# A Perceiver block on one Trainium2 core: the expert stage reordered, part of it moved into the last layer, and one exchange in the layers

## The reference, cut to what matters

```python
x = x + xattn(ctx, layernorm(x))
x = x + eight_layers(layernorm(x))        # attention part, then an MLP 512 -> 2048 -> 512, each with a layer norm
y = layernorm(x)
# 32 groups of 16 tokens; 64 experts (NE=16 times ES=4), each with 64 hidden units
logits = grouped(y) @ controller + tie
perm = (logits == max over the 16 tokens of a group)      # each expert picks one token of each group
sel = perm^T @ grouped(y)
inner = relu(sel @ f1 + bias)
inter = inner @ f2
out = perm @ inter                        # given back to the token that was picked
x = x + out
```

## Time and profile before

| | |
|---|---|
| median of 3 runs | 2298.01 us (2297.53 to 2298.12) |
| the profiled execution | 2295.51 us, of which the span from first to last instruction is 2293.7 us |
| PE busy | 94% of the span |
| DVE, ACT, POOL busy | 73%, 48%, 42% |
| mean granted TensorE clock | 0.984 of full speed |
| expert stage, first DVE instruction to the end | 2172.19 to 2293.7, 121.5 us |

### The profile page before, as it was taken

The page is one execution under the profiler, slowest core; times in us unless marked ns, Lnnn a source line. Parts: engine busy times, 40 slices in busy tenths (PEclk is TensorE's granted clock), DMA queues, the critical chain, the costliest instruction groups (busy, mean ns, idle before and its releaser), DMA issues. The chain is left out here.

```text
span 2293.7 us, 37795 instructions
## 1 busy us (share of the span) xinstructions
PE 2158.8 (94%) x12735; PEld 1091.0 (48%) x12735; DVE 1672.0 (73%) x2402; ACT 1101.9 (48%) x1720; POOL 969.0 (42%) x651
## 2 busy tenths in 40 slices
PE   5899999989999999998999999999999999999758
PEld 2444444433333333322475655657575665757333
DVE  7687777669999999999566757566675756666672
ACT  4122223234444545554564646556564655656343
POOL 0244344369999999876222204022221302122140
PEclk9999999999999999999999999999999999999979
DMA  3344544332432333321324232333423333332230
GB/s 116 134 141 145 180 142 156 128 111 86 131 103 83 119 108 106 112 81 56 122 93 133 94 115 84 129 102 117 132 74 111 101 117 96 129 120 86 84 111 19
DMA packets 159851, 252.71 MB, mean 110 GB/s; under 512 B 11506, under 2 KB 63986, under 8 KB 159730
## 3 DMA queue, kind: packets, MB, share of 16 engines
q1 hardware_dynamic: 159730, 250.96, 34.2%
HBM read 211.73 MB, written 36.70 MB: 108 GB/s over the span
## 5 line engine op out<-in xcount | busy, mean ns | idle before, releaser
L66 PE MATMUL l_mm<-l_xt_hi,wt_hi 128*128 128x256 f16 (+3 forms) x1568 | 413.8, 275 | 18.6 <-ACT hf L1691 11.5
L1335 POOL TENSOR_TENSOR l_rstd<-l_var_eps,neg_half 128x1 f32<-128x1 f32 x68 | 65.7, 966 | 839.1 <-DVE l_var_eps L1387 839.1
L67 PE MATMUL l_mm<-l_xt_lo,wt_hi 128*128 128x256 bf16 (+3 forms) x1568 | 413.5, 275 | 0.0
L68 PE MATMUL l_mm<-l_xt_hi,wt_lo 128*128 128x256 f16 (+3 forms) x1568 | 413.1, 275 | 0.0
L995 ACT ACTIVATE probs<-sc 128x1024 f32<-128x1024 f32 x272 | 275.7, 1023 | 251.7 <-PE sc L1086 197.8
L867 POOL TENSOR_TENSOR h_lo<-h_lo,probs 128x896 f32<-128x896 f32 x136 | 290.3, 2135 | 23.2 <-ACT probs L995 11.9
L867 POOL TENSOR_TENSOR wt_lo<-wt_lo,probs 128x896 f32<-128x896 f32 (+1 forms) x136 | 249.2, 1832 | 36.5 <-ACT probs L995 27.4
L1098 PE MATMUL pv<-probs,vb 128*64 128x512 f32 x1088 | 263.2, 605 | 0.0
L881 DVE TENSOR_REDUCE pmax<-mx 128x1024 f32 (+1 forms) x196 | 239.3, 1221 | 28.4 <-PE mx L1072 20.0
L68 PE MATMUL l_tok<-wt_hi,h_lo 128*128 128x512 f16 x576 | 218.3, 379 | 0.0
L1085 PE MATMUL sc<-q_hi,res 128*128 128x512 f16 x544 | 207.7, 382 | 9.2 <-ACT probs L995 7.2
(11 more groups left out here) (275 smaller groups left out, 3924.9 us busy)
## 6 DMA issues: line engine op xcount, KB each, us to landing
stage<-in_L_attn_Wf SPq DMA_DIRECT2D x64, 1024.0 KB, 5.2
keys<-wt_hi SPq DMA_DIRECT2D x136, 128.0 KB
res<-keys SPq DMA_DIRECT2D x68, 256.0 KB, 3.3
vb<-values SPq DMA_DIRECT2D x68, 256.0 KB, 5.6
stage<-in_ctx SPq DMA_DIRECT2D x16, 1024.0 KB, 9.8
values<-wt_lo SPq DMA_DIRECT2D x16, 1024.0 KB
stage<-in_L_ffn_f SPq DMA_DIRECT2D x16, 1024.0 KB, 5.3
res<-keys SPq DMA_DIRECT2D x68, 128.0 KB, 5.4
```

The costliest lines, as they stand in the source:

```text
L66: pe.matmul(out, lh, rh, start=first, stop=False, **kw)
L67: pe.matmul(out, lh, rl, start=False, stop=False, **kw)
L68: return pe.matmul(out, ll, rh, start=False, stop=last, **kw)
```

## The change

1. *Layers, all eight.* DVE does the biases of tiles 2 and 3 ahead of the low part of tile 1; ACT does gelu 2 ahead of the high part of tile 1; the four pieces of chunk F2+3 move on ACT behind `hidden(0)`, `hidden(1)` and `hidden(2)`.
2. *Last layer.* The transposes, high and low parts of tiles 0 to 2 are made there, of the stream normalised by a new `final_norm(t)`, and so are the high and low rows (`row_high`, `row_low`). The constants of the expert stage are loaded there too. Buffers are shared between stages for this (no instruction is added by that).
3. *Expert stage, head.* Only tile 3 is normalised, transposed and split. The logits come in two parts (tiles 0 to 2, then tile 3). The picks are copied by ACT, spread by POOL in two instructions a tile instead of by DVE in one; POOL clears tile 0's part ahead of that and the rest behind it.
4. *Second weights.* All eight low parts are POOL's, behind the clearing. ACT makes the high parts of chunks 4 to 7 between the quads 0, 2, 4 and 6.
5. *Back.* The transposes of the first eight quads stand inside the inner blocks, the copies of them on ACT too.
6. *Quads.* The selection is ordered so that a quad's rows 0 to 63 belong to tiles 0 and 1 and rows 64 to 127 to tiles 2 and 3. `expert_out` makes 32 output rows at a time, 12 products a quad; `give_back` uses 64 rows of the contraction in each of its eight products. The four stream tiles are added after all of them.

```diff
+LAST_F2 = {0: (0, 1), 1: (2,), 2: (3,)}
@@ layers_phase, DVE
+                def final_norm(t):
+                    dve.wait_ge(final_added, t + 1)
+                    tile_stats(stream_event(t), t, k.x_sb[:, t, :], EPS_OUTER)
+                    dve.wait_ge(rstd_done, stream_event(t) + 1)
+                    v.tensor_scalar(res[:, t, :], k.x_sb[:, t, :], mv[:, t, 0:1], rstd[:, t:t + 1],
+                                    ALU.subtract, ALU.mult).then_inc(normed, 1)
+                def row_low(t):
+                    dve.wait_ge(row_hi_done, t + 1)
+                    v.tensor_tensor(k.f_lo[:, t, :], res[:, t, :], k.f_hi[:, t, :], ALU.subtract).then_inc(row_lo_done, 1)
...
                     tile_shift(l, 1, bc_attn)
-                    low(m0 + 1, 1)
                     tile_bias(l, 2, attn_out[2], bc_attn)
                     tile_bias(l, 3, attn_out[3], bc_attn)
+                    low(m0 + 1, 1)
...
-                        if t and not last:
+                        if t:
                             low(m0 + TT + t - 1, t - 1)
+                        if t and last:
+                            row_low(t - 1)
...
+                            if t < TT - 1:
+                                final_norm(t)
@@ layers_phase, ACT
                     high(m0 + 0, 0)
+                    tile_gelu(l, 2)
                     high(m0 + 1, 1)
-                    tile_gelu(l, 2)
                     tile_gelu(l, 3)
-                    for n in range(4):
-                        chunk_piece(F2 + 3, n)
...
                         hidden(j)
+                        for n in LAST_F2.get(j, ()):
+                            chunk_piece(F2 + 3, n)
@@ layers_phase, PE
-                            if f == 10 and t and not last:
-                                transposes(m0 + TT + t - 1, t - 1)
+                            if f == 10 and t:
+                                transposes(m0 + TT + t - 1, t - 1, stream_event(t - 1) if last else None)
@@ expert_phase, SP
                 for m in range(2, 8):
-                    if 2 <= m < 6:
-                        sp.wait_ge(w_lo_pool, 4 * (m - 1))
-                    elif m >= 6:
-                        sp.wait_ge(w_lo_dve, 4 * (m - 5))
+                    sp.wait_ge(w_lo, 4 * (m - 1))
@@ expert_phase, POOL
-                g.memset(spread[:], 0.0).then_inc(cleared, 1)
+                clear(0)
+                for t in range(TT):
+                    spread_tile(t)
+                for t in range(1, TT):
+                    clear(t)
+                for m in range(8):
+                    weight_low(m)
@@ expert_phase, ACT
+                act.wait_ge(k.c_in, 48)
+                a.activation(ctl_hi[:], ctl[:], ACT.Copy).then_inc(ctl_hi_done, 1)
                 weight_high(0)
-                weight_high(1)
...
+                weight_high(1)
+                for b in range(BLOCKS_OF_PAIRS):
+                    back_copy(b)
                     act.wait_ge(inner_relu, b + 1)
                     a.activation(in_hi[:, 8 * b:8 * b + 8, :], inner[b % 2], ACT.Copy).then_inc(in_hi_done, 1)
-                    act.wait_ge(inner_ready, 4 * (b + 1))
-                    weight_high(4 + b)
+                    if b >= 2:
+                        weight_high(b)
+                for n in range(QUADS // 4, QUADS // 2):
+                    back_copy(n)
                 for q in range(QUADS):
...
                     a.activation(it_hi[q % 2], work[q % 2][:], ACT.Copy).then_inc(it_hi_done, 1)
+                    if q % 2 == 0 and q < 8:
+                        weight_high(4 + q // 2)
@@ expert_phase, PE
+                    if q % 2 == 0:
+                        pe.wait_ge(w_lo, 4 * (q // 2 + 1))
...
-                        x = product3(t_, work[q % 2][half * 64:(half + 1) * 64, :], (in_hi[:, pair, :], in_lo[:, pair, :]),
-                                     (wt_hi[:, m, n, :], wt_lo[:, m, n, :]), True, True)
+                        for a in range(2):
+                            rows, cols_ = slice(64 * a + 32 * half, 64 * a + 32 * half + 32), slice(32 * a, 32 * a + 32)
+                            x = product3(t_, work[q % 2][rows, :], (in_hi[:, pair, cols_], in_lo[:, pair, cols_]),
+                                         (wt_hi[:, m, n, :], wt_lo[:, m, n, :]), True, True,
+                                         tile_position=(0, rows.start))
...
-                    for t in range(TT):
-                        lhs = back[:, q, t * P:(t + 1) * P]
-                        t_.matmul(outs[t][:], lhs, it_hi[q % 2], start=q == 0, stop=False)
-                        x = t_.matmul(outs[t][:], lhs, it_lo[q % 2], start=False, stop=q == QUADS - 1)
+                    for part, it in enumerate((it_hi[q % 2], it_lo[q % 2])):
+                        for turn in range(2):
+                            for a in range(2):
+                                t = 2 * a + turn
+                                rows = slice(64 * a, 64 * a + 64)
+                                x = t_.matmul(outs[t][:], back(q)[rows, t * P:(t + 1) * P], it[rows, :],
+                                              start=q == 0 and part == 0,
+                                              stop=q == QUADS - 1 and part == 1)
```

More of the change, by code:

```diff
@@ L1712, in body @@
                             chunk_piece(F1 + t, n)
-                        if t and not last:
+                        if t:
                             high(m0 + TT + t - 1, t - 1)
+                        if t and last:
+                            row_high(t - 1)
                         tile_gelu(l, TT + t)
@@ L1890, in expert_phase, with back, packed @@
         outs = [pb(f"e_out{n}", [P, D], F32) for n in range(TT)]
-        c_in, staged = sem("e_c_in"), [sem(f"e_staged{n}") for n in range(2)]
+        logit_bank, pick_bank, bias_bank, tp_bank = outs
+        def back(q):
+            return back_early[:, q, :] if q < QUADS // 2 else back_late[:, q - QUADS // 2, :]
+        def packed(t):
+            return t[:].rearrange("p (e s g) -> p e s g", s=2, g=TILE_GROUPS)
+        staged = [sem(f"e_staged{n}") for n in range(2)]
         stats_done, mv_done, var_done, rstd_done, normed = (sem(n) for n in (
@@ L1936, in _, with clear, weight_low @@
                 g = nc.gpsimd
[L1937 to L1944 removed]
+                def clear(t):
+                    g.memset(spread[:, t, :, 1 - t // 2], 0.0).then_inc(cleared, 1)
+                    g.memset(spread[:, t, :, t // 2, :, 1 - t % 2], 0.0).then_inc(cleared, 1)
+                def weight_low(m):
                     pool.wait_ge(staged[m % 2], 16 * (m // 2 + 1))
@@ L1988, in _ @@
[L1988 to L1997 removed]
+                v.tensor_copy(bias_cols[:], bias_bank[:, 0:EP]).then_inc(bias_done, 1)
@@ new lines, in select @@
+                def select(t):
+                    pe.wait_ge(spread_done, 2 * t + 2)
+                    if t == LATE:
+                        pe.wait_ge(fr_lo_done, 1)
+                    for c in range(CH):
+                        n = CH * t + c
+                        if n >= 4:
+                            pe.wait_ge(sel_lo_done, n - 3)
+                        rhs = spread[:, t, :, t // 2, :, t % 2]
+                        out = work[n % 4][:].rearrange("p (q h n) -> p q h n", q=QUADS, h=2)
+                        t_.matmul(out, f_hi[:, t, c * P:(c + 1) * P], rhs, start=True, stop=False)
+                        t_.matmul(out, f_lo[:, t, c * P:(c + 1) * P], rhs, start=False, stop=True).then_inc(sel_ready, 1)
@@ L2131, in _ @@
                     x.then_inc(back_ready, 1)
+                pe.wait_ge(k.c_in, 48)
+                t_.transpose(bias_bank[:, 0:EP], k.bias_rows[:], k.ident[0:EP, 0:EP]).then_inc(bias_ready, 1)
+                pe.wait_ge(ctl_lo_done, 1)
+                logits_of(0)
+                pe.wait_ge(normed, 1)
+                for c in range(CH):
+                    x = t_.transpose(tp_bank[:, c * P:(c + 1) * P], f[:, LATE, c * P:(c + 1) * P], k.ident[:])
+                x.then_inc(tp_ready, 1)
@@ L2133, in expert_out @@
+                for n in range(QUADS // 4, QUADS // 2):
+                    back_transposes(n)
                 def expert_out(q):
+                    if q % 4 == 0:
+                        pe.wait_ge(in_lo_done, q // 4 + 1)
+                    if q % 2 == 0:
+                        pe.wait_ge(w_lo, 4 * (q // 2 + 1))
                     if q >= 2:
```

340 lines of the change are left out of this document (169 added, 171 removed).

## The result

The changed kernel takes 2260.54 us (median of 4 runs, 2255.57 to 2262.95), the kernel before on the same chip 2297.77 (2294.25 to 2298.12). The ratio is 0.984 with a 95% interval of 0.9822 to 0.9858: faster by 37.2 us. The forecast was 2262 in 2252 to 2276.

What follows compares the result with a forecast made beforehand. PE was taken to bound the layers, short chains, awaited weights and PE's quads the expert stage. Expert stage -36.5, last layer +9.4, layers -9.0 sum to -36.1: 2298.0 becomes 2261.9, predicted 2262 us, range 2252 to 2276.

Steps and rivals of the forecast that it cites:

- Layers, -9: Eight layers: PE's 1.44 us gelu wait goes, but tile 3's transposes lack slack; 1.1 gained a layer, bounds 0 to 11.5.
- rival D: Layers: the gain is eaten by tile 3's chain or ACT's later order, +9, 2271 us; chance 0.08.
- Last layer, +9.4: Last layer: PE stalls 2.7 us for the second norm plus transposes, 3.15 a tile, three tiles; bounds 1.4 to 12.
- Head, 9.4: Expert stage's start, up to the selection: 27.15 us becomes 9.4, -17.75; bounds 9 to 11.
- Selection, 12.2: Expert stage's selection: 11.86 us becomes 12.2; ACT gains one copy, PE starts at 1.2 GHz as before.
- Inner and back, 21.9: Expert stage's inner blocks and back transposes: 35.3 us becomes 21.9, -13.4; ACT's work sets the quads' start at 43.5.
- Quads, 36.3: Expert stage's sixteen quads: 43.3 us becomes 36.3, -7.0; 1.72 a quad, early ones held by ACT's queue and loads.
- the estimate of 0.84: Quads: `expert_out` would take 0.84 us by the skill's 3.07 times for four small tiles, making the whole 1.6 longer.
- B: Quads: small tiles overlap only partly: 64-row products not +7.4, 32-column products two at a time +5.7, both 2278 us; chance 0.17.
- E: Quads: small tiles run one after another, loads not hidden, 6.6 us a quad, kernel slower at 2332 us; chance 0.05.
- F: Quads: products serial, loads hidden, 4.52 us a quad, giving back what the rest gains, 2298 us; chance 0.04.
- rival C: Shorter: layers give all 11.5, head clock high, POOL 1.13 a piece: 2255 us, 2250 with half the stall; chance 0.08.

Runs made afterwards that it cites:

- e3: Changed kernel with only the layers' order of biases and gelu 2 (DVE and ACT) put back, weight pieces staying moved: 2271.81 us, ratio 0.9887.
- e2: Changed kernel with only the layers' weight pieces put back ahead of `hidden(0)` on ACT: 2261.29 us, ratio 0.984.
- e1: Changed kernel with both edits of the layers undone, on DVE and on ACT: 2270.81 us, ratio 0.9881.
- e5: Changed kernel with the last layer's transposes ahead of step 13 instead of step 10: 2257.19 us, ratio 0.9824.
- e9: Changed kernel with POOL clearing the first spread tile ahead of rstd instead of behind it: 2261.54 us, ratio 0.9844.
- e4: Changed kernel with `give_back` contracting all 128 rows instead of 64; 32-column products in `expert_out` kept: 2270.91 us, ratio 0.9879.
- e6: Changed kernel with ACT's weight chunks 6 and 7 moved from behind quads 4 and 6 to behind quads 6 and 9: 2259.0 us, ratio 0.9835.
- e7: Changed kernel with ACT's chunks 6 and 7 made in halves, two pieces behind each of quads 6 to 9: 2258.08 us, ratio 0.9828.
- e8: Changed kernel with 24 unused 512-column products added behind the layers' last product: 2259.88 us, ratio 0.9842.
- e13: Changed kernel with 29 unused products added behind the layers' last and 6 more ahead of the first logits: 2260.15 us, ratio 0.984.
- e11: Changed kernel with e5 and e7 together: 2251.3 us, ratio 0.9799.

## Why the prediction was right

Its mechanisms held, and nearly all its terms; the size came out with small errors that went both ways. The experiments undo or vary the layers, `give_back`, ACT's chunks and the last layer's stall. The two largest gains, head (17.7) and inner and back (12.6), no run undoes: for them the stretches of the two profiles stand alone.

- **Layers, -9.** PE's wait of 11.5 went, 3.4 came back at tile 3's transposes (4.4 less 1.0), and 0.8 less is waited elsewhere: 8.9, or 1.1 a layer as taken. Bias 0 is only 7.24 sooner, because the layers' first statistics are 0.63 later (1094.47 for 1093.84) and the clock behind them was lower (0.80 for 0.87), which the sum didn't have; like with like it is 8.8 to 9.0. The warning that tile 3 has no slack was the right one, and e3 shows it in full: rival D happens as soon as the order on DVE and ACT isn't changed too. Where I put the gain was half wrong: ACT's pieces ahead of `hidden(0)` looked like the cause, but moving them is neither needed (e2) nor enough (e3).
- **Last layer, +9.4.** Measured 9.8 (40.88 less 31.08). A tile grew by 2.70 instead of 3.15, as the stall is 2.07 and a little around it, not 2.7; that would be 8.1. The other 1.7 is the low clock in one of three tiles, which the sum didn't have. So that this term comes out is luck: a stall taken too long stood in for a low clock that was not foreseen, and with two such tiles, as in e1 and e3, it would be 11.5. In e5, where two waits of 0.93 are left, the low clock is gone.
- **Head, 9.4.** Measured 9.47, with the spread at 0.66 for 0.6 and the norm at 1.72 for the 0.55 used, which didn't matter, as e9 shows.
- **Selection, 12.2.** Measured 13.0: PE at 1.2 GHz for the first 5 us was slower than DVE's pace. The term's cover, "PE starts at 1.2 GHz as before", wasn't costed; it is 0.8 (in e9, where the clock rose sooner, the selection takes 11.8).
- **Inner and back, 21.9.** Measured 22.7.
- **Quads, 36.3.** Measured 35.2, but they began 1.7 later than forecast (45.2 behind the start for 43.5) and ended 0.6 later (80.4 for 79.8), because the loads and not the quads' beginning set their end. The chain through POOL's low parts and the loads came out closely: chunk 7 high at 64.3 behind the start (2239.01 less 2174.75) for 63.4, loads of 5.0 to 5.4, POOL 1.12 to 1.24 a piece. The steady period is 1.75 for 1.72. The 3.07 times and not four of the Trainium skill, TensorE: Matmul & The Clock Gate, Part 3, stands there for four tiles in rows, while `expert_out` has four in columns, so the estimate of 0.84 took it over to another kind; this trace shows no such loss, `expert_out` takes 0.65. Nor does a cost appear that would belong to a lost fast weight load (the Trainium skill, TensorEngine Tiling (Array Packing), Restrictions and Gotchas): the twelve loads hide behind twelve products.
- **End, 5.2.** Measured 5.2.

Expert stage 85.55 for 85.0; its start 2.56 later for 0.4 forecast. By spans the kernel gained 33.4 for 36.1. That the medians agree to 1.5 us while the spans miss by 2.7 is luck, of where the two profiled executions lie in their scatter.

Rivals B, E and F fell with the period of 1.75; e4 prices half of B at 8.6 in the quads and 10.4 in the medians (7.4 worked out). Of rival C two things came in part, the shorter stall (2.06 for 2.7) and POOL's 1.12 a piece in chunks 4 to 7; the layers' whole 11.5 and a high clock in the head did not.

What stays open: why the load in e5 was late; what decides which tiles of the last layer get the low clock, and whether one or two; why the clock in the layers' first 26 us is 0.87 in some executions and 0.80 in others; and what the gaps without a releaser amid the small inner products are.

## What to carry to other kernels

A wait for one engine often covers a second, nearly as long, for another: ask which is next, and move that too; an edit that takes away only the first (e3) gives nothing. Before two profiles are subtracted, compare the granted clock of the same stretch in both: here it hid a microsecond of the layers' gain and added 1.7 to two of the experiments. A queue that converts weights between steps of a chain should take small pieces, no sooner than the load has surely landed: ACT standing before a load held up the intermediates (e6, e7). And put a new wait where its input is nearly there: three steps later brought 6.2 us of waits down to 1.9 and gave 5 us in the last layer, 1.7 of it through the clock (e5).

## What the hardware showed that I had not expected

- Twelve products of 32 output rows and 512 columns in 0.65 us, 0.22 for four: four column groups overlap entirely.
- A VectorE norm of 0.55 takes 1.72 beside a GpSimd memset of 0.96 and 0.53; it takes 0.55 without it (e9).
- Three waits of 2.06 us, one a tile, and TensorE's clock dips in one tile of the three (0.88), the middle or the last from kernel to kernel, and in the first and the last in e1 and e3; with two waits of 0.93 (e5, e11) in none.
- Two gaps of 1.16 and 1.27 us, and the products behind them ran at 1.2 GHz (e8); with none over 0.3 they ran at 2.4 (e13).
- A clock won at one place was lost at the next: with the selection at 0.90 (e9) the start of the inner blocks fell to 0.73, and the quads began 0.2 sooner than in the changed kernel, where the selection had 0.77.
- In a stream of 64-column products 0.03 apart PE stood for up to 1.90 us with nothing that the profile names (e13); eight other kernels have 0.6 to 1.8 us of it in two gaps there, and e1, e3, e5 and e9 none.
